# Router logits from zero-padded sliding weights, a single-pass list product and filler matmuls in a three-part transformer tower

## What is computed

```python
h = tok_ref(x, ...)                      # attention-free mixer, 32 x 256 tokens of width 256
h = concat([cls_tok, h], axis=1)         # 257 tokens an image
h = h + attn_ref(layernorm(h), ...)      # 16 heads, low-rank projections
z = layernorm(h)                         # 8224 tokens
shared = silu(z @ w1.T) * (z @ w2.T) @ w3.T          # hidden 1024
scores = sigmoid(z @ router_w.T)                     # 8 experts
top_idx = top_k(scores + expert_bias, 2)
gates  = scores * one_hot(top_idx).sum(-2)
routed = sum over the two experts of gate * expert(z)    # hidden 256 each
out = h + shared + routed
```

## Time and profile before

| | us |
|---|---|
| median of 3 runs | 2326.11 |
| lowest and highest | 2321.05, 2334.31 |
| profiled execution, its own time | 2322.05 |
| span in its profile | 2320.2 |
| around the span | 1.85 |

### The profile page before, as it was taken

The page is one execution under the profiler, slowest core; times in us unless marked ns, Lnnn a source line. Parts: engine busy times, 40 slices in busy tenths (PEclk is TensorE's granted clock), DMA queues, the critical chain, the costliest instruction groups (busy, mean ns, idle before and its releaser), DMA issues. The chain is left out here.

```text
span 2320.2 us, 42607 instructions
## 1 busy us (share of the span) xinstructions
PE 2135.5 (92%) x15706; PEld 1856.2 (80%) x15706; DVE 1413.9 (61%) x3029; ACT 1006.7 (43%) x2076; POOL 687.9 (30%) x737
## 2 busy tenths in 40 slices
PE   5899999989999998999986899989999999999998
PEld 4677777767777777777764899989999888889998
DVE  7566666666666666766653454477664444444776
ACT  2145454554545455454544333322223555554332
POOL 4324232332323233232210211100002333333766
PEclk9799999999999999999998899999999999999999
DMA  2423424243342323224230533200002333333665
GB/s 78 74 50 74 72 56 77 51 83 57 70 77 51 78 55 80 64 64 77 42 66 18 190 119 129 77 28 29 28 19 80 103 104 104 105 106 102 185 184 157
DMA packets 125273, 189.24 MB, mean 82 GB/s; under 512 B 23153, under 2 KB 76418, under 8 KB 125074
## 3 DMA queue, kind: packets, MB, share of 16 engines
q1 hardware_dynamic: 101232, 134.65, 24.7%
q0 software_dynamic: 12736, 34.69, 5.2%
q10 hardware_dynamic: 11106, 17.19, 2.3%
HBM read 84.32 MB, written 49.58 MB: 58 GB/s over the span
## 5 line engine op out<-in xcount | busy, mean ns | idle before, releaser
L835 DVE TENSOR_REDUCE mx<-ps 128x2 f32<-128x514 f32 x512 | 350.9, 685 | 184.3 <-PE ps L467 184.3
L665 ACT ACTIVATE pT<-ps 128x514 f32<-128x514 f32 x512 | 306.7, 601 | 356.2 <-PE ps L484 351.4
L467 PE MATMUL ps<-km,q 112*128 112x258 f32 x1024 | 262.8, 338 | 102.4 <-DVE mx L835 90.4
L467 PEld LDWEIGHTS ps<-km,q 112*128 112x128 f32 x1024 | 162.4, 191 | 200.6 <-DVE mx L835 141.8
L1974 POOL DMA_INDIRECT z<-zd,itab x136 | 129.2, 950 | 484.4 <-DVE itab L1887 268.4
L484 PE MATMUL ps<-q,km 114*128 114x258 f32 x1024 | 227.5, 305 | 3.1 <-ACT pT L665 3.1
L1271 PE MATMUL ps<-zhi,whi 128*128 128x256 f32 x1056 | 217.8, 288 | 4.0 <-DVE wlo L1914 3.9
L1271 PE MATMUL ps<-zhi,wlo 128*128 128x256 f32 x1056 | 213.9, 284 | 0.0
L1271 PE MATMUL ps<-zlo,whi 128*128 128x256 f32 x1056 | 213.5, 284 | 0.0
L1299 ACT ACTIVATE sil<-ps 128x512 f32<-128x512 f32 x132 | 79.0, 598 | 280.4 <-PE ps L1271 280.4
L484 PEld LDWEIGHTS ps<-q,km 114*128 114x128 f32 x1024 | 161.2, 192 | 45.6 <-ACT pT L665 35.4
(11 more groups left out here) (318 smaller groups left out, 4983.9 us busy)
## 6 DMA issues: line engine op xcount, KB each, us to landing
yd<-raws SPq DMA_DIRECT2D x136, 128.0 KB, 1.8
q<-qhi SPq DMA_DIRECT2D x128, 129.0 KB, 4.2
km<-khi SPq DMA_DIRECT2D x256, 64.5 KB, 3.2
xs<-in_x SPq DMA_DIRECT2D x64, 256.0 KB, 4.4
z<-hscr SPq DMA_DIRECT2D x46, 256.0 KB, 2.9
raws<-in_wu SPq DMA_DIRECT2D x12, 768.0 KB, 4.7
hscr<-h SPq DMA_DIRECT2D x34, 256.0 KB, 5.1
zd<-z SPq DMA_DIRECT2D x33, 256.0 KB, 2.0
```

The source lines that it names most:

```text
L467: last = pe.matmul(ps[:, k, 0:NP], q2[p % U][0:MAXROW, QAT[g], t * P:(t + 1) * P], km[p % 2][0:MAXROW, k, g, :], start=True, stop=True)
L665: act.activation(pT[:, 2 * g:2 * g + 2, t, :], ps[:, score_bank(b, n):score_bank(b, n) + 2, 0:N], ACT.Exp, scale=HD ** -0.5).then_inc(s_ok, 1)
L835: dve.tensor_reduce(mx[:, t, 2 * QAT[g]:2 * QAT[g] + 2], ps[:, 0:2, 0:N], AX_X, ALU.max, negate=True).then_inc(mx_ok, 1)
```

## The change

1. **Logits.** The router weights, high part in 8 columns and low part in 8 more, stand in the middle of a zeroed tile `rww` of 2 x 240 columns. For block number j of a group, a 128-column slice of it that begins at 112 - 16 j is the stationary operand, and the 256 tokens of the block stream past it. So block j's 16 results land on partitions 16 j to 16 j + 15, the other rows get zeros added, and up to eight blocks accumulate in one 128 x 256 tile of bank 5. Four matmuls a block (`zhi`, `zlo`, two halves of the width) replace twelve. There are five groups of 7, 8, 8, 8 and 2 blocks. When one is complete, ACT copies it (`copy_logits`, at `u` = 3 of every odd `k`, and at `k` = 8, `u` = 0), PE turns it in two transposes (`turn_logits`, at `u` = 0 of the next even `k`, and at `k` = 8, `u` = 1), and DVE adds high and low results in three or four small reductions (`gather_logits`, in the same step). The first block of a group waits until the group before has been copied. The tanh is one instruction from SBUF at `k` = 8, `u` = 2 in place of two from PSUM at `u` = 1.
2. **List.** The one-hot tiles become float32r (`hots`), with the codes shifted by 4096 so that they fit, and the shift is added back where `itab` is read.
3. **Fillers.** In stage A one filler after each head's scores of image 31, four in each of four gaps of the last step, and 8, 1 and 14 behind the class-token matmuls; in stage B 24 with 128 columns before the first turn and 24 after it.
4. Small things: a memset of `rww` on DVE ahead of the one that begins stage B, three semaphores merged into one, the raw router weights in `acc`.

```diff
@@ stage A, PE
                     scores(b, p, 2 * n + 1)
+                    if b == B - 1 and n > 0:
+                        filler(0, 1)
...
                         turn_values(b - 1, n - 1)
+                        if b == B:
+                            filler(0, 4)
...
+                    if n in (3, 4) and b == B:
+                        filler(0, 4)
...
         last.then_inc(ot_ps, 1)
+        filler(0, 8)
...
         last.then_inc(onT_ps, 1)
+        filler(0, 1)
...
         pe.matmul(ps[:, 7, 0:D], ro[:, 0:P], wos[:], start=True, stop=True).then_inc(o_ps, 1)
+        filler(0, 14)
@@ stage B, PE
             def logits(k, p):
-                for t in range(LT if k < B else 1):
-                    at = (k * LT + t) * NE
-                    dst = ps[:, 5, at:at + NE] if at < BANK else ps[:, 7, 0:NE]
-                    mm = [(z_, w_, f) for z_, w_ in ((zhi, rwh), (zlo, rwh), (zhi, rwl)) for f in range(FT)]
...
+                g = next(g for g in range(GROUPS) if k in members[g])
+                at = LEFT - RW * sorted(members[g]).index(k)
+                if k == members[g][0] and g > 0:
+                    pe.wait_ge(lgc_ok, g)
+                mm = [(z_, f) for z_ in (zhi, zlo) for f in range(FT)]
+                for n, (z_, f) in enumerate(mm):
+                    last = pe.matmul(ps[:, 5, 0:L], rww[:, f, at:at + P], z_[p][:, f, :],
...
+            def turn_logits(g):
+                pe.wait_ge(lgc_ok, g + 1)
+                if g > 0:
+                    pe.wait_ge(lge_ok, g)
+                for t in range(LT):
+                    last = pe.transpose(ps[:, 7, t * P:(t + 1) * P], lgT[:, t * P:(t + 1) * P], eye[:])
                 last.then_inc(lg_ps, 1)
...
+            pe.wait_ge(rt_step, 1)
+            filler(24)
             turn(pe, 0)
+            filler(24)
...
+                    if (k, u) in LOGITS_AT:
+                        turn_logits(LOGITS_AT.index((k, u)))
@@ stage B, ACT
+            def copy_logits(g):
+                act.wait_ge(lg_ps, 2 * g + 1)
+                act.activation(lgT, ps[:, 5, 0:L], ACT.Copy).then_inc(lgc_ok, 1)
...
-                    if k == X1 - 1 and u == 1:
-                        act.wait_ge(lg_ps, K)
+                    if (k, u) in LOGITS_OUT:
+                        copy_logits(LOGITS_OUT.index((k, u)))
+                    if k == X1 - 1 and u == 2:
+                        act.wait_ge(lge_ok, GROUPS)
                         act.wait_ge(w_lo, NU)
-                        act.activation(sc[:, 0:BANK], ps[:, 5, :], ACT.Tanh, scale=0.5).then_inc(th_ok, 1)
-                        act.activation(sc[:, BANK:WIDE], ps[:, 7, 0:NE], ACT.Tanh, scale=0.5).then_inc(th_ok, 1)
+                        act.activation(sc, raw_lg[:, 0:WIDE], ACT.Tanh, scale=0.5).then_inc(th_ok, 1)
@@ stage B, DVE
+            def gather_logits(g):
+                dve.wait_ge(lg_ps, 2 * g + 2)
...
+            dve.memset(rww[:].bitcast(F32), 0.0)
             dve.memset(ones[:].bitcast(F32), 1.0).then_inc(rt_step, 1)
...
+                    if (k, u) in LOGITS_AT:
+                        gather_logits(LOGITS_AT.index((k, u)))
@@ the list
-    hot_p = [raws[:, WIDE + n * PICK * P:WIDE + (n + 1) * PICK * P] for n in range(2)]
+    hots = nc.alloc_sbuf_tensor_at("hots", [P, 2 * PICK * (P + NQ)], F32R, offset=raws_at + 4 * WIDE)
+    hot_p = [hots[:, n * PICK * P:(n + 1) * PICK * P] for n in range(2)]
...
-                    dve.tensor_copy(itab[:], ps[:, 5, 0:NQ]).then_inc(list_ok, 1)
+                    dve.tensor_scalar(itab[:], ps[:, 5, 0:NQ], CENTRE, None, ALU.add).then_inc(list_ok, 1)
```

More of the change, by code:

```diff
@@ L601, in _ @@
             last = pe.matmul(ps[:, 6, f:f + 1], clsz[:, f * P:(f + 1) * P], one1[:], start=True, stop=True)
-        last.then_inc(clsT_ps, 1)
+        last.then_inc(cls_ps, 1)
         pe.wait_ge(clsT_ok, 1)
@@ L605, in _ @@
             last = pe.matmul(ps[0:3 * HARM, 5, 16:17], basT[:, f, :], zT[:, f, CLS:N], start=(f == 0), stop=(f == FT - 1))
-        last.then_inc(clsr_ps, 1)
+        last.then_inc(cls_ps, 1)
         pe.wait_ge(clsr_ok, 2)
@@ L1142, in stage_b @@
     wlo = sb("wlo", [P, NU, UW], F32R)
+    raws_at = -(-nc.sbuf_base // 32) * 32
     raws = sb("raws", [P, RAW * UW])
+    assert nc.sbuf_base == raws_at + 4 * RAW * UW
     raw = [raws[:, u * UW:(u + 1) * UW] for u in range(RAW)]
-    rwr = sb("rwr", [P, FT * NE])
-    rwh = sb("rwh", [P, FT, NE], F32R)
-    rwl = sb("rwl", [P, FT, NE], F32R)
+    RW = 2 * NE
+    LEFT = P - RW
+    rww = sb("rww", [P, FT, LEFT + P], F32R)
     ebias = sb("ebias", [P, NE])
@@ L1169, in stage_b @@
     acc = sb("acc", [P, LT, D])
-    one = [sb("hit%d" % c, [P, WIDE]) for c in range(TOP)]
+    hits = [sb("hit%d" % c, [P, K * LT * NE]) for c in range(TOP)]
+    one = [t[:, 0:WIDE] for t in hits]
     key, tmp, sum_a, sum_b, sc = (raws[:, n * WIDE:(n + 1) * WIDE] for n in range(5))
@@ L1217, in stage_b @@
     EXTRA = K - X1
+    GROUPS = (X1 + 1) // 2
+    members = [[] for g in range(GROUPS)]
+    for k in range(X1):
+        xs = ([NX * k - 1] if k > 0 else []) + ([NX * k, NX * k + 1] if NX * k < EXTRA else [])
+        members[k // 2] += [k] + [X1 + j for j in xs]
+    LOGITS_AT = [(2 * g + 2, 0) for g in range(GROUPS - 1)] + [(X1 - 1, 1)]
+    LOGITS_OUT = [(2 * g + 1, 3) for g in range(GROUPS - 1)] + [(X1 - 1, 0)]
+    raw_lg = hits[0]
+    lgT = one[1][:, 0:L]
     held = [len(range(p, EXTRA, NX)) for p in range(NX)]
@@ L1560, in logits @@
             def logits(k, p):
-                for t in range(LT if k < B else 1):
-                    at = (k * LT + t) * NE
-                    dst = ps[:, 5, at:at + NE] if at < BANK else ps[:, 7, 0:NE]
-                    mm = [(z_, w_, f) for z_, w_ in ((zhi, rwh), (zlo, rwh), (zhi, rwl)) for f in range(FT)]
-                    for n, (z_, w_, f) in enumerate(mm):
-                        last = pe.matmul(dst, z_[p][:, f, t * P:(t + 1) * P], w_[:, f, :], start=(n == 0),
-                                         stop=(n == len(mm) - 1))
+                g = next(g for g in range(GROUPS) if k in members[g])
[5 more added lines that the diff above has]
+                    last = pe.matmul(ps[:, 5, 0:L], rww[:, f, at:at + P], z_[p][:, f, :],
+                                     start=(n == 0 and k == members[g][0]),
+                                     stop=(n == len(mm) - 1 and k == members[g][-1]), skip_group_check=True)
+                if k == members[g][-1]:
+                    last.then_inc(lg_ps, 1)
+            def turn_logits(g):
[4 more added lines that the diff above has]
+                    last = pe.transpose(ps[:, 7, t * P:(t + 1) * P], lgT[:, t * P:(t + 1) * P], eye[:])
                 last.then_inc(lg_ps, 1)
@@ L1591, in places, with filler @@
                 pe.matmul(ps[:, 6, NE:2 * NE], ones[:], mask[:, BANK:WIDE], start=True, stop=True).then_inc(pos_ps, 1)
+            def filler(count):
+                for i in range(count):
+                    pe.matmul(ps[:, 2, 0:P], ones[:], ones[:], start=True, stop=True)
+            pe.wait_ge(rt_step, 1)
+            filler(24)
             turn(pe, 0)
+            filler(24)
             for k in range(XN):
@@ L1668, in _ @@
             act.wait_ge(b_load, 16 * (len(consts) + 1))
-            act.activation(rwh[:].rearrange("p f e -> p (f e)"), rwr[:], ACT.Copy).then_inc(r_hi, 1)
+            act.wait_ge(rt_step, 1)
+            act.activation(rww[:, :, LEFT:LEFT + NE], rwr, ACT.Copy).then_inc(r_hi, 1)
             act.activation(earlier[:], acc[:, 0, 0:P], ACT.Copy).then_inc(r_hi, 1)
@@ L1738, in chain @@
                 dve.wait_ge(rt_step, count[0])
+            def gather_logits(g):
+                dve.wait_ge(lg_ps, 2 * g + 2)
+                order = sorted(members[g])
+                runs = [[k for k in order if k < X1], [k for k in order if k >= X1]]
+                for run in runs:
+                    j, n = order.index(run[0]), len(run)
+                    for t in range(LT):
+                        m = n - 1 if t == 1 and run[-1] == B else n
+                        if m > 0:
+                            cols = raw_lg[:, run[0] * LT * NE:(run[0] + m) * LT * NE].rearrange("p (b t e) -> p b t e", t=LT, e=NE)
+                            last = dve.tensor_reduce(
+                                cols[:, :, t, :],
+                                ps[:, 7, t * P + RW * j:t * P + RW * (j + m)].rearrange("p (b s e) -> p b e s", s=2, e=NE),
+                                AX_X, ALU.add)
+                last.then_inc(lge_ok, 1)
             def best(c):
@@ L1916, in _ @@
             dve.wait_ge(r_hi, 2)
-            dve.tensor_tensor(rwl[:].rearrange("p f e -> p (f e)"), rwr[:], rwh[:].rearrange("p f e -> p (f e)"),
-                              ALU.subtract).then_inc(r_lo, 1)
+            dve.tensor_tensor(rww[:, :, LEFT + NE:LEFT + RW], rwr, rww[:, :, LEFT:LEFT + NE], ALU.subtract).then_inc(r_lo, 1)
             norm_x(1)
@@ L2073, in layout @@
     row = row[:, :B * LT + 1]
```

(2 more changed lines are left out.)

27 lines of the change are left out of this document (15 added, 12 removed).

## The result

| | before | after |
|---|---|---|
| median of four runs each, us | 2324.1 | 2267.84 |
| lowest and highest | 2321.05, 2334.31 | 2265.89, 2268.15 |
| profiled execution, own time / span | 2322.05 / 2320.2 | 2268.15 / 2266.3 |

Lines have moved: logits are line 1595, the list 1619, `hidden` 1298, `output` 1315, the turning 1607.

A forecast was written before the change was run, and what follows sets the result against it. PE was taken to bound the logits and list stretches. From 2322.05 us, 24.8 - 1.45 + 1.5 + 16.2 + 1.1 (fillers) = 42.2 came off, giving 2279.9; half of 4.1 added made 2282, range 2272 to 2293.

The forecast's parts named there:

- The logits: Stage B router matmuls: four of 0.118 us replace twelve of 0.107 per block; gain 23.7 + 1.1 = 24.8 us.
- the routing: Stretch after the logits where DVE decides: tanh one step later costs nothing, at most 0.5 us.
- 2 us for the median: Whole kernel: half of the 4.1 us by which the profiled execution lay under the median, added to the forecast.
- The turning: New transposes of each logit group and the slower pair behind them: 0.29 us a group, 1.45 us in all.
- `k` = 0: First step of stage B: weight units set the pace, so PE waits before `hidden(0, 2)`; only the third block's 0.8 us stays.
- The dip: Only clock dip between 1300 and 1755 us, following the 8-column matmuls: 1.5 us gained, between 0 and 1.7.
- The list: One-hot products from 1580 to 1755 us: one float32r record each, 130 at 0.105 us; gain 16.2 us.
- the rival that lets the columns pace the list: List: weight loads hide fully, 0.063 us a product, gain 21.7 us, total 2276; chance 0.05.
- the seam's: Between stages A and B: clock stays down, fillers overflow by 8.3 us, their 1.1 not gained, total 2291; chance 0.12.
- The x stream: Logits stretch: x loads cannot keep up, a `k` stays at 24.2 us, total 2306; chance 0.03.

The follow-up runs named there:

- c_w0: Changed kernel with `rww` inside `mask`, `whi` at byte 0 and `zhi`, `hhi` at byte 64 of a 128-byte line; 2268.37 us.
- c_split: Changed kernel with `rww` inside `mask`, `whi` and `zhi` at byte 96 of a 128-byte line, `hhi` at byte 32; 2275.9 us.
- a_nofill: Changed kernel without any of the fillers that the change adds, in stage A and stage B; 2269.72 us.
- c_64_less: `c_64` without the 48 fillers in stage B and the last 14 of stage A; 2268.06 us.
- a_noshift: Changed kernel with `rww` allocated last in stage B and small tiles in its place, so the tiles behind stand at their old places; 2278.01 us.
- c_64: Changed kernel with `rww` inside `mask`, `whi` at byte 96 and `zhi`, `hhi` at byte 32 of a 128-byte line; 2265.85 us.
- c_0: Changed kernel with `rww` inside `mask`, `whi`, `zhi` and `hhi` all at byte 0 of a 128-byte line; 2279.67 us.
- c_32: Changed kernel with `rww` inside `mask`, `whi` at byte 96 and `zhi`, `hhi` at byte 0 of a 128-byte line; 2279.35 us.
- c_96: Changed kernel with `rww` inside `mask`, `whi` at byte 96 and `zhi`, `hhi` at byte 64 of a 128-byte line; 2272.45 us.

## Why the prediction was right in direction and missed the size

- **The step that failed** is the assumption, under *The logits* and in every sum, that `hidden` and `output` go on at 2.84 and 1.43 us. I listed the larger `rww` as a thing that costs DVE a memset and did not ask what else it moves. At the old places the changed kernel makes the sum: from image 29's residual on it gains 44.4 - 2.1 = 42.3 us, against 42.2. That it does so to 0.1 us is luck: the parts are off by -0.2, +1.9, -0.6, -0.5 and -0.4, and cancel. The new places are worth 10.2 us by the medians, 9.2 by the profiles: 2.1 in the logits, 4.5 in the list, 4.5 from the routed tiles on, less 1.7 for a dip in the routing, 0.2 ahead. No rival of mine had this mechanism, so the range could not hold it. The other 5 us between 2282 and 2267.84 are mostly the chance gain of 2.8 before image 29 and the 2 us of the next point.
- **Adding 2 us for the median** was wrong in sign. What lifts the other runs of the kernel before above its first profile goes mostly with the granted clock, as the 35 runs above show, and the changed kernel has no dip in its logits: its runs lie within 2.3 us, and its profiled one is the highest.
- **The logits**: right in kind. 132 records, 0.47 us for a block of four as costed in the rows below and 0.49 on the mean, no wait before the transposes, a `k` of 20.5 to 20.7 us ("about 21"). The gain at the old places is 25.6, not 23.75. Summed from start to start over the records between the two products, the router matmuls give 23.1; the turns of the blocks take 9.9 in place of 11.1 (0.35 in place of 0.41 us behind logits, which I had not counted); `hidden` and `output` give 2.0, the dip included; the new transposes cost 0.7.

```profile
1439.80 0.40 PE L1595 MATMUL ps<-zhi,rww 128*128 128x256 f32 x2
1440.04 0.40 PE L1595 MATMUL ps<-zlo,rww 128*128 128x256 f32 x2
1440.27 0.60 PE L1583 MATMUL ps<-eye,z 128*128 128x128 f32 x4
1440.62 0.48 PE L1298 MATMUL ps<-zhi,whi 128*128 128x256 f32 x2
...
1454.70 0.38 PE L1607 MATMUL ps<-eye,hit 128*128 128x128 f32 x2
1454.84 0.49 PE L1595 MATMUL ps<-zhi,rww 128*128 128x256 f32 x2
1455.16 0.40 PE L1595 MATMUL ps<-zlo,rww 128*128 128x256 f32 x2
```

- **The turning**: two transposes 0.14, the pair behind them 0.32 in place of 0.23: 0.23 a group, 1.15 in all, where I had 0.29 and 1.45. PE waits for no copy.
- **`k` = 0**: as forecast, PE comes early to `hidden(0, 2)` and waits for POOL, here 1.33 us:

```profile
1292.80 3.47 POOL L2075 TENSOR_TENSOR wlo<-raws,whi 128x1536 fp32r<-128x1536 f32 x1 [3.38 <-ACT whi L1709]
...
1296.37 0.47 PE L1298 MATMUL ps<-zhi,whi 128*128 128x256 f32 x2 [1.33 <-issue]
```

- **The dip**: the 1.5 us and their bound of 1.7 were my estimate from the stretch at 0.83, 10 x (1 - 0.83) = 1.7. In the profile before, the four windows of 1 us from 1391 to 1395 have 0.75, 0.50, 0.50 and 0.54, and from product to product such a dip was measured at 1.49 us; but how many there are is chance. I also wrote that no clock below 1.00 would be left up to the list's end; there are two, both in the routing, where PE is not full. One, 0.83 at 1490 to 1500 us, is there in `c_w0`, `c_split`, `a_nofill` and `c_64_less` too, and not in `a_noshift`, `c_64`, `c_0`, `c_32` and `c_96`. It makes about 1.4 of the -2.3 of the routing, for which I had allowed 0.5: that much more `c_64_less` takes there than `c_64`, which differs in fillers alone. The other lies at 1530 to 1550 us (0.74 and 0.92). All ten kernels with the new logits have it, and so have three of the four profiles with the old ones, at 1560 to 1580; only the first profile of before has none. The rest of the -2.3 was not traced.
- **The list**: 130 records at 0.10 us (four in 0.40), forecast 0.105; 15.7 and 16.1 us in the two kernels with the old places, forecast 16.2. So the rival that lets the columns pace the list, at 0.063 a record, falls: of the 20.2 us of the changed kernel some 4 lie in `hidden` and `output`.
- **The rivals**: the seam's did not come as a whole (the slices at the end of stage A read 9, and its last store is issued at 1269.73 us against 1276.01), but half of its sign did: the first `hidden` begins at half clock, at 0.43 us for two matmuls, and the clock is 0.66 at 1280 to 1290 us. The x stream kept up (a `k` of 20.5 to 20.7 us).

## What to carry to other kernels

A change that resizes one tile moves all that are allocated behind it, and an unchanged matmul may run at another pace for that alone (here 1728 bytes, and `hidden` at 2.799 us in place of 2.865): compare the tiles' addresses before a gain is put down to an edit, and undo the move as an experiment of its own. Where PE decides, it is worth a try to place moving operands 64 bytes, modulo 128, from their weights: here it was worth 2% of `hidden` and `output`, some 10 us of 2278, but next to nothing in the routed part (353.8 us against 354.2). And a dip of the clock seen once in a profile is a draw (four profiles with the same logits had 1, 6, 3 and 5 stretches with one): ask how often it could have come before it is priced.

## What the runs showed of the hardware

- A stream of float32r matmuls with 128 stationary and 256 moving columns takes 0.119 us each with the operands 0 bytes apart (modulo 128) and 0.117 with 64, both as means that include the slower first pair behind a transposition; at 64 streams of 0.113 and of 0.118 alternate. The same work takes 2278.01 us with 0 and 2267.84 with 64 (`a_noshift` and after). By what means the distance sets the pace no run here shows.
- With matmuls of 8 moving columns in it, a stream in which PE is busy all the time had its granted clock at 0.66 to 0.97 in 1 to 6 of 19 stretches of 10 us. With products of 256 columns in their place it stayed at 1.00 from 1310 to 1480 us in all ten profiles.
- The part from block 21's last product to block 22's first, with the routed tiles in it, takes 352.7 to 356.8 us in kernels that differ only in where tiles stand (`c_split` and `c_w0`). What decides there was not tried.
